# Writing out the loops of attention and of the experts' stage, with every wait on a constant

## The reference, cut to what matters

```
x = x + experts(x)      # 8 experts, top 2 of 8 by a softmax, and a shared one (2 x 128 wide)
x = x + attention1(x)   # 16 heads of 64, one shared key and value head, bias by distance (Toeplitz)
x = x + attention2(x)   # the same, bias read from an input of 16 x 1024 x 1024
x = x + attention3(x)   # as attention1, other weights

# each attention, for b in 2, head h in 16, row i in 1024:
sim  = q[b,h,i] . k[b,j] * scale + bias[h,i,j]     # j: a null key first, then j <= i
out  = softmax(sim) @ v[b]                         # causal
y    = layernorm(concat_heads(out) @ Wout)

# experts: y += w[t,e] * (leaky(x @ gate_e) * (x @ up_e)) @ down_e
```

## Time and profile before

| | |
|---|---|
| device time, median of three | 2221.59 us |
| the profiled execution | 2221.87 us |
| its span, first to last instruction | 2220.1 us |
| TensorE busy | 1971.5 us (89%) |
| VectorE, ScalarE, GpSimd busy | 77%, 60%, 48% |
| mean granted TensorE clock | 0.940 of 2.4 GHz |
| attention, first exponential to last, layers 1, 2, 3 | about 440, 455 and 428 us |

### The profile page before, as it was taken

How to read it: one execution, slowest core, us unless ns; L and a number is a source line. 1 busy time by engine, 2 the same in 40 slices (tenths; PEclk the granted TensorE clock), 3 DMA queues, 4 the chain that set the end, 5 groups by cost and what they waited for, 6 DMA issues and landing times. The chain is left out here.

```text
span 2220.1 us, 48620 instructions
## 1 busy us (share of the span) xinstructions
PE 1971.5 (89%) x12082; PEld 1439.7 (65%) x12082; DVE 1708.9 (77%) x4092; ACT 1339.0 (60%) x2911; POOL 1067.6 (48%) x1307
## 2 busy tenths in 40 slices
PE   5999586999999998689999999986795999999988
PEld 4888463666666667566666666665563666666668
DVE  4777877788887785757788787858577888888857
ACT  2222665677776674246677666644564777777754
POOL 0443213566765562405566656524023666766643
PEclk8999698899999999798999999998796999999999
DMA  3631068233333343286787777752366334433333
GB/s 118 206 101 41 28 211 280 91 115 114 117 121 106 114 162 112 77 306 201 226 245 244 238 231 231 236 178 77 101 230 193 105 122 122 128 124 114 114 115 115
DMA packets 248203, 338.94 MB, mean 153 GB/s; under 512 B 28838, under 2 KB 154924, under 8 KB 248012
## 3 DMA queue, kind: packets, MB, share of 16 engines
q1 hardware_dynamic: 248012, 336.87, 47.8%
HBM read 250.62 MB, written 102.91 MB: 159 GB/s over the span
## 5 line engine op out<-in xcount | busy, mean ns | idle before, releaser
L1687 POOL TENSOR_SCALAR at_row<-at_row,at_inv 128x769 f32<-128x769 f32 (+7 forms) x384 | 697.9, 1818 | 381.2 <-DVE at_inv L1849 372.9
L1894 ACT ACTIVATE at_row<-at_row,at_nmax 128x769 f32<-128x769 f32 (+7 forms) x768 | 594.7, 774 | 279.4 <-DVE at_nmax L1868 272.3
L1868 DVE CUSTOM_DVE_ANT_0 at_row<-at_s,bias,at_row 128x768 f32<-128x768 f32 (+7 forms) x768 | 610.1, 809 | 81.0 <-PE at_s L1797 39.3
L1809 PE MATMUL at_t<-ident,at_row 128*128 128x128 f32 x3456 | 532.0, 281 | 8.3 <-DVE at_pt L1698 6.5
L1809 PEld LDWEIGHTS at_t<-ident,at_row 128*128 128x128 f32 x3456 | 391.6, 142 | 217.1 <-issue 167.4
L1796 PE MATMUL at_s<-k_hh,q_hl 128*128 128x512 f32 (+3 forms) x1152 | 464.1, 403 | 47.9 <-SPq L1754 23.3
L1824 PE MATMUL at_o<-at_pt,v 128*64 128x256 f32 (+3 forms) x2688 | 460.8, 459 | 1.7 <-DVE at_pt L1698 1.7
L1797 PE MATMUL at_s<-k_lp,q_h 65*128 65x512 f32 (+3 forms) x1152 | 394.6, 354 | 0.0
L1889 ACT ACTIVATE at_pt<-at_t 128x512 f32<-128x512 f32 (+2 forms) x576 | 307.8, 535 | 100.7 <-PE at_t L1809 96.3
L1698 DVE COPY at_pt<-at_t 128x384 f32<-128x384 f32 (+3 forms) x576 | 279.5, 485 | 113.1 <-PE at_t L1809 110.8
L1687 DVE TENSOR_SCALAR at_row<-at_row,at_inv 128x769 f32<-128x769 f32 (+7 forms) x384 | 285.8, 744 | 1.7 <-issue 0.6
(11 more groups left out here) (249 smaller groups left out, 2834.0 us busy)
## 6 DMA issues: line engine op xcount, KB each, us to landing
q_dram<-o_in SPq DMA_DIRECT2D x76, 512.0 KB, 3.8
bias<-bands_dram SPq DMA_DIRECT2D x64, 512.0 KB, 5.8
q_hl<-q_dram SPq DMA_DIRECT2D x96, 256.0 KB, 4.0
q_hl<-q_dram SPq DMA_DIRECT2D x192, 128.0 KB, 3.0
bands_dram<-brow_dram SPq DMA_DIRECT2D x2, 8192.0 KB, 32.8
bias<-corners_dram SPq DMA_DIRECT2D x256, 64.0 KB, 3.4
bias<-in_fside SPq DMA_DIRECT2D x32, 448.0 KB, 3.6
q_h<-q_dram SPq DMA_DIRECT2D x48, 256.0 KB, 4.6
```

Of the source, the lines that this page charges most:

```text
L1687: return eng.tensor_scalar(cells(u), cells(u), inv[:, u % RING:u % RING + 1], None, ALU.mult)
L1809: last = eng.transpose(t_ps[m % NTR][:, c * P:(c + 1) * P], weights(u)[:, here:here + P], t["ident"][:])
L1868: eng.tensor_tensor_reduce(out=weights(u), in0=s_ps[u % 2][:, 0:width], in1=bt[:, lo:lo + width], scale=-1.0, scalar=null_cell(u)[:, 0:1], ...
L1894: eng.activation(cells(u), cells(u), ACT.Exp, scale=-1.0, bias=nmax[:, i:i + 1], accum_out=rsum[:, i:i + 1]).then_inc(s["exp"], 1)
```

## The change

Every loop in these two stages becomes a Python loop, so that each engine's stream is one straight line; all turns are numbers. The waits and addresses are constants by that. The `gate` increments and the semaphore go. The order of the work on every engine, its tiles and its transfers stay. The two small `if`s that place the split of the output weights in turn 3 of the first half are reworded so that they still fall there.

```diff
@@ run_halves
     for half in range(B):
-        with eng.Fori(0, turns - 1) as turn:
+        for turn in range(turns if half < B - 1 else turns - 1):
             steps(half, turn, late, size + late, lambda n, per: True)
-        if half < B - 1:
-            steps(half, turns - 1, late, size + late, lambda n, per: True)
     steps(B - 1, turns - 1, late, size + late, peeled(B * turns - 1))
@@ run
-    with eng.Fori(0, turns - 1) as turn:
+    for turn in range(turns - 1):
         steps(turn, late, size + late, lambda n, per: True)
@@ moe_experts, SP and GpSimd
-                with eng.Fori(0, NU // PAR - 1) as it:
+                for it in range(NU // PAR - 1):
@@ moe_experts, mask_corners and split
-                    eng.sem_inc(s["gate"], 1)
@@ attend, SP
-                with eng.Fori(1, TURNS) as turn:
-                    loads(place(0, turn), False)
-                for half in range(1, B):
-                    with eng.Fori(0, TURNS) as turn:
-                        loads(place(half, turn), False)
+                for turn in range(1, B * TURNS):
+                    loads(place(turn // TURNS, turn % TURNS), False)
@@ attend, ScalarE (and GpSimd with n % 6 == 2 and 14 <= n < 38)
-                    if turn.known() and 0 <= turn.turn < TURNS and turn.half < B - 1 and n % 6 == 0 and 12 <= n < 36:
+                    if turn.turn == TURNS - 1 and turn.half < B - 1 and n % 6 == 0 and 12 <= n < 36:
                         out_weights(n // 6 - 2)
```

More of the change, by code:

```diff
@@ L421, in moe_experts @@
     CORNERS = H // (NU // PAR - 1)
-    names = ["w_in0", "w_in1", "gate", "w_split", "w_hi", "gu", "slope", "leaky", "hidden", "hid_hi", "hid_lo", "down",
+    names = ["w_in0", "w_in1", "w_split", "w_hi", "gu", "slope", "leaky", "hidden", "hid_hi", "hid_lo", "down",
              "added"] + [f"corner_{n}{j}" for n in ("in", "masked", "out") for j in range(CORNERS)]
@@ L1645, in attend @@
                  ev_d=NPC // 2, pv=NGRP, out=NGRP)
-    names = list(marks) + ["q0", "q1", "gate", "wo_in", "wo_hi", "wo_lo", "o0", "o1"] + [f"bias{n}" for n in range(NBIAS)]
+    names = list(marks) + ["q0", "q1", "wo_in", "wo_hi", "wo_lo", "o0", "o1"] + [f"bias{n}" for n in range(NBIAS)]
     def slot_loads(n):
@@ L1952, in step @@
                 def step(turn, n, has):
-                    if turn.known() and 0 <= turn.turn < TURNS and turn.half < B - 1 and n % 6 == 2 and 14 <= n < 38:
+                    if turn.turn == TURNS - 1 and turn.half < B - 1 and n % 6 == 2 and 14 <= n < 38:
                         low_weights(n // 6 - 2)
```

## The result

The changed kernel takes 2183.18 us (median of 4 runs, 2182.66 to 2183.8) beside 2222.45 (2221.52 to 2224.15, 4 runs) for the kernel before: ratio 0.9823, interval 0.9806 to 0.984. It is 39.3 us faster. The forecast was 2174 and 47.4 us. Two of the three mechanisms held; the term of layer 2 was too large, and the term of the experts' copies had the wrong cause. 2183.2 is inside the range of 2160 to 2192, but just above 2182, which the prediction itself named as its forecast's upper end.

The account below looks back on a forecast made before the run. The prediction took TensorE, busy 89% of 2220.1 us, to bound the kernel unless something starves it. Its terms summed as 2221.87 - 14.85 - 2.95 - 26.2 - 3.4 = 2174.5, forecast as 2174 us, range 2160 to 2192.

Parts of the forecast that it names:

- Term 1: Attention, layers 1 and 3: VectorE's loop-end stalls and the clock dip go when written out; gains 14.85 and 2.95 us.
- Term 2: Attention, layer 2: SP's issue of transfers sets the pace; written out, it falls below TensorE's 53.5 us; gain 26.2 us.
- 0.5 us a turn as residue: Layer 2: allowance for queuing bursts of transfers once SP's issue is shorter, 7 x 0.5 us taken off the gain.
- Term 3: Experts: three looped copies of 16 token weights take 1.05 us and hold up TensorE; removing this gains 3.4 us.
- Edits at nothing: `gate` increments and register arithmetic on TensorE, ScalarE and GpSimd are hidden, valued at 0; more code to fetch, 0.
- Rival A: Written-out turns: straight code is not fetched in time, two naked stops a turn, 24 turns lose 72 us, 2246; chance 0.04.
- rival B: Layer 2 stays transfer-bound; its gain is only 6 us, giving 2195, or 0, giving 2200; chance 0.11.
- C: Attention turns: the constants do shorten the turn, by 0.5 us, giving 2164; chance 0.14.
- D: VectorE's loop ends are slow for another reason that stays, a memory access; layers 1 and 3 gain nothing, 2192; chance 0.03.
- the upper end of 2182: Whole kernel: the forecast's upper end, with half of the clock dips' 6 us back and 2 more of residue.

Follow-up runs that it names:

- The ring run: The changed kernel with layer 2's bias rows' places laid out once over all 256 units of a layer: 2172.83 us, ratio 0.9787.

## Why the prediction was right, and where it was not

Term 1, VectorE's loop end: right in cause and size, 15.5 us for 14.85 in layer 1 and 3.2 for 2.95 in layer 3 (turns 1 to 6 alone gave 14.8, the pair of layer 3 2.9). It held because the measure was taken from an undisturbed pair of the same kernel, so that the clock dip was counted with the stall that caused it.

Term 2, SP in layer 2: right in cause, the largest error in size, 18.0 us for 26.2 (17.0 in turns 1 to 7, which the term counts, the rest in turn 0). The step that failed is "What is late next? ... I leave 0.5 us a turn as residue". SP's issue did fall to 0.95 us a row, but the next in line was neither TensorE nor the transfers. It was a wait of SP's own, on the free space of the bias rows, which costs 1.8 us a turn where I took 0.5 (12.7 us over seven turns; 0.9 to 1.8 a turn over the runs with this layout). The ring run shows it: with that wait gone the turns take 53.5. I listed how long the issue takes and how full the DMA engines are, but not the lead at which each transfer may be issued; that stands in L63 to L79 and needs no trace. The 12.6 us of the earlier trace rows were waits of just this kind, on VectorE's reading, the longest 5.3, and I read them only as a sign that SP was never short of work.

Term 3, the experts' token weights: nothing that can be shown for 3.4. Layer 1's first exponential came 1.2 us earlier, but it came at 391.8 to 392.6 too in the three runs that leave the experts looped, and the three long copies are still there. The step that failed is its cause. "Removed: three turns at 1.15" took the register address for the reason of the 1.05 us, because the short copy in the written-out last turn had a constant one. That turn differs in a second thing too: no masks run in it. Five of the eight looped copies had a register address and took 0.17, which spoke against that cause from the start.

Edits at nothing: the gates and the register arithmetic of the three other engines are worth nothing in turns that TensorE bounds (107.0 to 107.1 before and after). Alone, the latter even cost 7 us, in layer 2 only; in the whole change it does not show, presumably since there SP has the room. The remaining 1.5 us between the layers is not attributed.

The sum: 39.3 us measured against 47.4. Term 2's miss of 8.2 and term 3's of 2.2 (counting its 1.2) are partly made good by 0.9 in term 1 and the 1.5 elsewhere. Rival A did not appear in the whole change, rivals B, C and D each fell to a run. Two things in the prediction don't carry weight: the upper end of 2182 does not follow from the two parts named for it, which reach about 2179, so that the range held is in part due to rival B's 2195 that widened it; and the two costs it names in SP's loop, the 0.2 us a row and the 3 us of the loop end, were never parted by a run.

## What to carry to other kernels

Compare equal work in unequal time within one profile: the best stretch is the measure, and what the slower ones lack in PE busy time has a place that can be looked up. When a queue's issue time is taken off, look next at the lead of each of its waits (how many units before the load the space was last read), and at the worst of them, not the mean; a layout that starts again each turn has its worst at the seam. Before an operation's odd duration is put down to its operands, look what the other engines do in the same microsecond.

## What the runs showed of the hardware

A loop of VectorE's with some 300 instructions stalls at its end for 2.8 to 3.1 us or for 0.3, and which it is depends on where its code lies; 50 instructions more in front swap the stalling ends for others. In layer 2, with the DMA engines at some 0.75, the stall took 4.4 to 5.4 us. Where no end stalled, the loops of all engines ran 108 us of layer 1 without one packet of instructions; where VectorE's stalled, ten were fetched in 111 us. SP's loop, some 320 instructions in layer 2, stalls alike: 3.0 us at each end in one half, 0.3 in the other.

A copy of 16 numbers a partition by VectorE took 1.06 us instead of 0.17 beside an affine select of 1.42 us on GpSimd, and ended with it.

Semaphore increments are not free ahead of a stage's first work: 100 of them ran for 9.2 to 9.6 us on VectorE's queue and put the attention off by 3.5 to 7.6 us, where the gates inside a TensorE-bound stage showed no cost.
